# Placing 50,000 edges with one-hots of eight columns, columns innermost, in a four-layer graph network on one core

## The chip, the cores and the metric

The kernel runs on one core of a Trainium2 chip. The metric is the device time of one execution in microseconds (us), the median of several runs. TensorE (PE) multiplies matrices into PSUM, and its weight loads are listed as PEld; VectorE is DVE, ScalarE ACT, GpSimd POOL, SyncE SP.

## The reference

Four layers run on 3,125 nodes with 128 features and 50,000 edges (src, dst), edges sorted by dst. Each layer normalizes x, applies relu, gathers over edges and adds its result to x. Layers 0, 1 and 2 need the mean over incoming or outgoing edges, which this kernel takes from a dense count matrix A of the edges; layer 3 needs an attention over edges in both directions.

```python
msgs = x[row]
summed = jax.ops.segment_sum(msgs, col, num_segments=num_nodes)
count = jax.ops.segment_sum(jnp.ones((row.shape[0],), x.dtype), col, num_segments=num_nodes)[:, None]
agg = summed / jnp.maximum(count, 1.0)
...
edge_index = jnp.stack([src, dst])
h = jnp.maximum(_layernorm(x, axis=-1), 0.0)
x = x + _L0_gnn_ref(h, L0_gnn_W_lin, L0_gnn_W_agg, edge_index)
```

## The kernel before, in words

To build A, the edges are first sorted into 50 cells (25 tiles of 128 sources by two bands of 1,600 destinations). The input holds them as 125 partitions of EC = 400 columns. `place_dve` works out for each edge its place: a chunk number (0 to 447, `sort_v[:, 0]`) and a row in the chunk (0 to 127, `sort_v[:, 1]`), and two payloads of it, the destination and the source inside the cell, each plus one (`sort_v[:, 2]` and `[:, 3]`).

The stage of the change, "permute", moves the payloads to those places by matmuls. For every one of the 400 edge columns the weights are a one-hot of the row (128 wide) times a payload, the moving operand is a one-hot of the chunk (448 wide), and the product adds into PSUM bank 4 for one payload and bank 5 for the other: 800 matmuls of 448 columns in all, with 125 rows.

`permute_dve` handles U0 = 4 columns as a group. Per column it writes the chunk's one-hot into `A0` (L487, a comparison of `steps_h` with a per-partition scalar); for three columns (ACT_COLS) it writes the row's one-hot alone into `eq0` (L489); for the fourth it writes both products itself into `B0` (L492). `permute_act` multiplies the other three one-hots by both payloads (L513). `permute_pe` runs the group's eight matmuls (the helper `add_to`, L537). Operands of one column lie packed, and there are four buffers of each (g).

The signals: VectorE raises `eq_ready` after a group, ScalarE then `payload_ready`, TensorE `perm0_used` after its eight matmuls. VectorE waits for `perm0_used` of four groups before. After the last one it reads both banks (L502, L503) and raises `sorted_ready`, which opens the next stage, "build" (L558, L566, and L537 again), which makes A. There `oh_s` already holds eight columns innermost, made by one comparison (L566), and TensorE takes its weights from it as `oh_s[s][:, :, j]`, one f16 number in 16 bytes.

While the stage starts, GpSimd still runs `norm` for layer 0 with six instructions on the whole of h (L935 to L944). No DMA runs inside the stage.

Four lines elsewhere are read below for what they show of an access: L1251, a matmul whose moving operand `mrb[d][:, :, :, k]` takes 24 bf16 numbers from 24 rows of 416 or 448; L1176, a sum of two f32 results from bf16 columns of `sE`, 12 numbers (24 bytes) apart; L1374, a copy that writes `exs` 12 numbers apart; L1068, the same number of values in runs of 12. L739 is a packed cast of 1,024 numbers like L1375, and the matmuls of `exs` have 12 packed moving columns.

Of the kernel before, what the change touches and what calls it, by code (L numbers as in the profile page):

```python
# [7 lines left out]
F16 = mybir.dt.float16  # L8
BF16 = mybir.dt.bfloat16
I32 = mybir.dt.int32  # L10
ALU = mybir.AluOpType
ACT = mybir.ActivationFunctionType
AX_X = mybir.AxisListType.X

P = 128
# [4 lines left out]
EP = 125  # L20
EC = N_EDGES // EP
# [11 lines left out]
def chunk_bound(buckets):  # L33

    lap = LAP * GROUP
    return -(-((N_EDGES + buckets * (P - 1)) // P) // lap) * lap


CH = tuple(chunk_bound(b) for b in BUCKETS)
CHUNKS = max(CH)  # L40
# [48 lines left out]
def linker(eng, sem):  # L89

    count = [0]

    def link(ins):
        count[0] += 1
        ins.then_inc(sem, 1)
        eng.wait_ge(sem, count[0])

    return link


def gnn_kernel(nc, edges, x_in, consts, steps, weights, bias_cols, bias_rows, attn, out):
    with ExitStack() as ctx:
        def sb(name, shape, dt=F32):
            return ctx.enter_context(nc.sbuf_tensor(name, shape, dt))

        def sem(name):
            return ctx.enter_context(nc.semaphore(name))
# [5 lines left out]
        PS = ctx.enter_context(nc.psum_tensor("PS", [P, 8 * BANK], F32))  # L113
# [40 lines left out]
        exs = sb("exs", [P, 2, GROUP, SPLIT * HEADS], BF16)  # L154


        U0 = 4
        ACT_COLS = 3
        arena = sb("arena", [P, 29600])

        def view(at, width, rows=P):
            return arena[0:rows, at:at + width]
# [10 lines left out]
        def three(a):  # L173
# [13 lines left out]
        steps_h = view(26400, BW // 2).bitcast(F16)  # L187
        tabs = view(27200, CHUNKS + CELLS, 1).bitcast(I32)
        cell_turn, cell_end = tabs[:, 0:CHUNKS], tabs[:, CHUNKS:CHUNKS + CELLS]
        sort_v = view(23200, 4 * EC, EP).rearrange("p (a b) -> p a b", a=4)  # L190
# [1 line left out]
        packed = view(28800 + EC, EC, EP).bitcast(I32)  # L192
        back_i = view(28512, CH[0]).bitcast(I32)

        A0 = [view(g * U0 * CHUNKS // 2, U0 * CHUNKS // 2, EP).bitcast(F16).rearrange("p (j c) -> p j c", j=U0)
              for g in range(4)]
        B0 = view(3584, 16 * P, EP).bitcast(F16).rearrange("p (g j k c) -> p g j k c", g=4, j=U0, k=2)
        eq0 = view(5632, 8 * P, EP).bitcast(F16).rearrange("p (g j c) -> p g j c", g=4, j=U0)
        dst_in = view(6656, CH[1])

        RING_D, RING_S, RING_A = 4, 2, 4
# [2 lines left out]
                for s in range(RING_S)]  # L204
        stage = [view(11424 + s * BW // 2, BW // 2).bitcast(F16) for s in range(RING_A)]

        iota_8 = view(14624, GROUP * P // 2).bitcast(F16).rearrange("p (c j) -> p c j", j=GROUP)
        key_h = view(14624 + GROUP * P // 2, CHUNKS // 2).bitcast(F16)

# [65 lines left out]
        prod_ready, prod_used = sem("prod_ready"), sem("prod_used")  # L275
        placed, addr_ready = sem("placed"), sem("addr_ready")
        eq_ready, payload_ready, perm0_used = sem("eq_ready"), sem("payload_ready"), sem("perm0_used")
        sorted_ready = sem("sorted_ready")
        pads_written, scattered, order0_here = sem("pads_written"), sem("scattered"), sem("order0_here")
        order0_ready = sem("order0_ready")  # L280
# [56 lines left out]
        dve_link = linker(nc.vector, dve_step)  # L337
# [137 lines left out]
                t.matmul(PS[0:EP, SORT:SORT + EC], ident[0:EP, 0:EP], prod[:, n % PROD, :], start=(n == 0),  # L475
                         stop=(n == BUCKETS[d] - 1), skip_group_check=True).then_inc(prod_used, 1)

        LAPS0 = EC // (4 * U0)

        def permute_dve(v):  # L480

            def group(i, g, first=False):
                if not first:
                    v.wait_ge(perm0_used, 4 * i + g - 3)
                for j in range(U0):
                    c = bass.ds((4 * i + g) * U0 + j, 1)
                    v.tensor_scalar(A0[g][:, j, :], steps_h[0:EP, 0:CH[1]], sort_v[:, 0, c], None, ALU.is_equal)  # L487
                    if j < ACT_COLS:
                        last = v.tensor_scalar(eq0[:, g, j, :], steps_h[0:EP, 0:P], sort_v[:, 1, c], None, ALU.is_equal)  # L489
                    else:  # L490
                        for k in range(2):
                            last = v.tensor_scalar(B0[:, g, j, k, :], steps_h[0:EP, 0:P], sort_v[:, 1, c],  # L492
                                                   sort_v[:, 2 + k, c], ALU.is_equal, ALU.mult)
                last.then_inc(eq_ready, 1)

            for g in range(4):
                group(0, g, True)
            with v.Fori(1, LAPS0) as i:
                for g in range(4):
                    group(i, g)  # L500
            v.wait_ge(perm0_used, 4 * LAPS0)
            v.tensor_scalar(key[:, 1, :], PS[:, 5 * BANK:5 * BANK + CH[1]], -1.0, None, ALU.add)  # L502
            v.tensor_scalar(dst_in, PS[:, 4 * BANK:4 * BANK + CH[1]], -1.0, None, ALU.add).then_inc(sorted_ready, 1)  # L503

        def permute_act(a):

            with a.Fori(0, LAPS0) as i:
                for g in range(4):
                    a.wait_ge(eq_ready, 4 * i + g + 1)
                    for j in range(ACT_COLS):  # L510
                        for k in range(2):
                            c = bass.ds((4 * i + g) * U0 + j, 1)
                            last = a.activation(B0[:, g, j, k, :], eq0[:, g, j, :], ACT.Copy, scale=sort_v[:, 2 + k, c])  # L513
                    last.then_inc(payload_ready, 1)

        def permute_pe(t):
            for k in (4, 5):
                clear_bank(t, k)
            with t.Fori(0, LAPS0) as i:
                for g in range(4):  # L520
                    t.wait_ge(payload_ready, 4 * i + g + 1)
                    for j in range(U0):
                        for k in range(2):
                            at = (4 + k) * BANK
                            last = add_to(t, PS[:, at:at + CH[1]], B0[:, g, j, k, :], A0[g][:, j, :])
                    last.then_inc(perm0_used, 1)

        def clear_bank(t, k, n=BANK):
            t.matmul(PS[:, k * BANK:k * BANK + n], zeros[:, 0:P], zeros[:, 0:n], start=True, stop=False,
                     skip_group_check=True)  # L530
# [5 lines left out]
        def add_to(t, where, lhsT, rhs):  # L536
            return t.matmul(where, lhsT, rhs, start=False, stop=True, skip_group_check=True)  # L537
# [948 lines left out]
        def _(v):  # L1486
# [6 lines left out]
            v.wait_ge(loaded_steps, 16)  # L1493
            v.nop().then_inc(placed, 1)
            permute_dve(v)
            build_dve(v)

# [114 lines left out]
        def _(t):  # L1612
# [15 lines left out]
            place_sum_pe(t, 1, 0, CELLS)  # L1628
            t.wait_ge(placed, 1)
            permute_pe(t)  # L1630
            build_pe(t)
            t.wait_ge(slot_free, BANDS + CELLS)
# [93 lines left out]
        def _(a):  # L1726
            a.wait_ge(wx_summed, 1)
            a.copy(Wx[:, :], PS[:, 6 * BANK:6 * BANK + SC]).then_inc(wx_ready, 1)
            norm_act(a, 0)
            a.wait_ge(placed, 1)  # L1730
            permute_act(a)
            build_act(a)
            a.wait_ge(h_ready, 1)
# [105 lines left out]
```

## Time and profile before

| | us |
|---|---|
| three runs | 3679.42, 3669.36, 3679.49 (median 3679.42) |
| the profiled execution | 3675.2 |
| its span | 3673.1 |
| PE busy | 2217.1 (60%) |
| DVE busy | 2275.1 (62%) |
| ACT busy | 834.8 (23%) |
| POOL busy | 1652.6 (45%) |
| L513, 600 products | 186.1 busy |
| L487, 400 comparisons of 448 | 160.2 busy |
| L537, 4,320 matmuls of several stages | 781.0 busy |

The profile is of one execution. Busy is the time in which an engine had an instruction under way; instructions of one engine overlap at their ends, so a duration is longer than the distance from one to the next. A line number is that of the kernel before.

### The profile page before, as it was taken

To read this page: it belongs to the slowest core of one execution; us is meant where nothing else is said; L and a number is where in the kernel's file an instruction comes from. 1 tells how busy PE (TensorE), PEld (TensorE's weight loads), DVE (VectorE), ACT (ScalarE), POOL (GpSimd) and SP (SyncE) were. 2 spreads that over 40 slices of the span, in tenths; PEclk is the share of its full clock that TensorE was granted. 3 is DMA by queue.
4 is the path that set the end of the run, shared out by engine and by line. 5 is a ranking of instruction groups with operands and counts; after the bars stand their busy time and mean duration, and the time that the engine had idled before them with its cause. 6 is when DMAs were issued, how large, how long until landed. Compare 5 with 4: busy or idle time off the path is not lost.

```text
span 3673.1 us, 46525 instructions
## 1 busy us (share of the span) xinstructions
PE 2217.1 (60%) x12603; PEld 1303.9 (35%) x12659; DVE 2275.1 (62%) x3122; ACT 834.8 (23%) x1389; POOL 1652.6 (45%) x1455
## 2 busy tenths in 40 slices
PE   0688777778968999857333333334557554336663
PEld 0333545544534555524311111112456211115563
DVE  8999888885497003532233334337577896349877
ACT  0198333320012001120000100002334221004442
POOL 7300333330477777740266666657644666630000
PEclk9799999999979999979555555555589897555797
DMA  2000111114434342044433333332367333320352
GB/s 65 0 0 0 45 45 45 45 40 135 125 108 117 87 100 42 1 96 102 67 90 89 91 93 90 90 86 74 88 206 232 101 88 96 88 48 0 107 176 85
DMA packets 195114, 301.51 MB, mean 82 GB/s; under 512 B 120540, under 2 KB 133818, under 8 KB 194922
## 3 DMA queue, kind: packets, MB, share of 16 engines
q1 hardware_dynamic: 138986, 175.88, 15.1%
q0 software_dynamic: 40512, 62.87, 9.2%
q10 hardware_dynamic: 15552, 61.94, 5.6%
q8 instruction: 36, 0.59, 0.1%
q14 instruction: 28, 0.23, 0.0%
HBM read 191.65 MB, written 88.01 MB: 76 GB/s over the span
## 4 chain that ended last, share of the span: by engine, by line
PE 28%; DMA 24%; issue 17%; DVE 15%; POOL 9%; ACT 5%; ACTq 0%; DVEq 0%; SPq 0%; POOLq 0%; PEldq 0%
DMA arena<-T_att,idx 23%; PE PS L537 10%; POOL arena L1304 9%; PE PS L698 6%; PE PS L883 6%; ACT arena L513 3%; DVE arena L558 3%; PE PS L972 3%; DVE arena L1195 1%; DVE arena L373 1%; PE PS L475 1%; DVE arena L489 1%; PE PS L959 1%; DMA T_att<-parts 0%; DVE arena L566 0%
## 5 line engine op out<-in xcount | busy, mean ns | idle before, releaser
L1304 POOL DMA_INDIRECT arena<-T_att,idx x864 | 843.2, 976 | 627.8 <-DMA arena<-T_att,idx 457.5
L537 PE MATMUL PS<-arena 128*128 128x400 f16 (+2 forms) x4320 | 781.0, 331 | 266.1 <-issue 106.0
L1139 DVE TENSOR_REDUCE arena<-PS 128x1024 f32 (+1 forms) x432 | 504.7, 1216 | 582.5 <-PE PS L1106 562.3
L537 PEld LDWEIGHTS PS<-arena 128*128 128x128 f16 (+2 forms) x4320 | 528.3, 158 | 509.1 <-issue 350.0
L1477 POOL DMA_INDIRECT order<-arena x400 | 513.3, 1283 | 252.4 <-issue 252.4
L1095 PE MATMUL PS<-ident_b,score_buf 128*32 128x128 bf16 x864 | 96.2, 279 | 552.9 <-ACT score_buf L1068 542.0
L1106 PE MATMUL PS<-arena,pick 128*128 128x512 bf16 x812 | 340.5, 525 | 139.7 <-DVE arena L1139 107.1
L558 DVE TENSOR_SCALAR arena<-arena 128x1600 f16<-128x1600 f16 x448 | 381.1, 896 | 59.8 <-PE PS L537 55.6
L698 PE MATMUL PS<-arena 128*128 128x512 f16 (+1 forms) x1575 | 318.7, 362 | 95.5 <-issue 82.1
L632 POOL TENSOR_TENSOR rdeg<-rdeg,arena 128x1600 f32<-128x1600 f32 x48 | 160.1, 3337 | 307.0 <-ACT arena L616 307.0
L1095 PEld LDWEIGHTS PS<-ident_b,score_buf 128*32 128x32 bf16 x864 | 71.3, 124 | 625.3 <-issue 554.7
L698 PEld LDWEIGHTS PS<-arena 128*128 128x128 bf16 x1575 | 148.0, 99 | 262.2 <-issue 111.2
L513 ACT ACTIVATE arena<-arena 125x128 f16<-125x128 f16 x600 | 186.1, 388 | 79.0 <-DVE arena L492 73.6
L1106 PEld LDWEIGHTS PS<-arena,pick 128*128 128x128 bf16 x864 | 65.3, 111 | 362.1 <-DVE arena L1139 279.7
L1241 PE MATMUL PS<-ident_b,arena 128*128 128x128 bf16 x864 | 110.8, 309 | 134.5 <-issue 76.4
L1351 DVE TENSOR_TENSOR arena<-PS,key 128x1024 f32<-128x1024 f32 x108 | 132.3, 1225 | 90.5 <-PE PS L537 82.9
L1068 ACT COPY score_buf<-h 128x96 bf16 (+1 forms) x52 | 14.1, 271 | 665.8 <-POOL h L1313 665.8
L487 DVE TENSOR_SCALAR arena<-arena 125x448 f16<-125x448 f16 x400 | 160.2, 417 | 0.5 <-PE PS L537 0.5
L1273 ACT COPY arena<-PS 128x1024 bf16<-128x1024 bf16 x108 | 109.1, 1012 | 208.1 <-PE PS L1241 160.4
L883 PE MATMUL PS<-arena 128*128 128x400 f16 x800 | 147.0, 337 | 10.8 <-DVE arena L860 8.8
L616 ACT CAST arena<-PS 128x1600 f16<-128x1600 f32 x50 | 74.6, 1492 | 339.7 <-PE PS L537 339.7
L972 PE MATMUL PS<-arena,W 128*128 (+1 forms) x384 | 136.3, 514 | 20.9 <-DVE arena L1002 10.2
(258 smaller groups left out, 2797.6 us busy)
## 6 DMA issues: line engine op xcount, KB each, us to landing
spill<-arena SPq DMA_DIRECT2D x108, 560.0 KB
arena<-spill ACTq DMA_DIRECT2D x108, 560.0 KB
arena<-A SPq DMA_DIRECT2D x50, 800.0 KB
A<-arena SPq DMA_DIRECT2D x50, 400.0 KB, 2.4
arena<-A SPq DMA_DIRECT2D x50, 400.0 KB
arena<-T_att,idx POOLq DMA_INDIRECT x864
order<-arena POOLq DMA_INDIRECT x400
T_att<-h SPq DMA_DIRECT2D x2, 1600.0 KB, 13.9
```

What stands on the lines that cost most here:

```text
L487: v.tensor_scalar(A0[g][:, j, :], steps_h[0:EP, 0:CH[1]], sort_v[:, 0, c], None, ALU.is_equal)
L513: last = a.activation(B0[:, g, j, k, :], eq0[:, g, j, :], ACT.Copy, scale=sort_v[:, 2 + k, c])
L537: return t.matmul(where, lhsT, rhs, start=False, stop=True, skip_group_check=True)
L558: v.tensor_scalar(oh_d[s], steps_h, dst_in[:, bass.ds(RING_D * i + s, 1)], None, ALU.is_equal) \
L698: last = t.matmul(PS[:, a0:a1], narrow[s][:, k, :], strips[g % RING][:, a0:a1], start=(k == 0 and s == 0), stop=(k == TILES - 1 and s == S ...
L883: last = t.matmul(PS[:, at:at + w], wide[c][s][:, k, :], halves[n % HALVES][:, q * w:(q + 1) * w], start=(k == 0 and s == 0), stop=(k == T ...
L972: last = t.matmul(o, wt(name, c * H1 + ob * P), rhs, start=(n == 0), stop=(n == len(terms) - 1))
L1095: last = t.transpose(bank[:, j * P:(j + 1) * P], score_buf[:, half, j, :], ident_b[:, :])
L1106: last = t.matmul(PS[:, hd * BANK:(hd + 1) * BANK], pick[:, hd, :], sT[:, s:s + QUAD, :].rearrange("p j e -> p (j e)"), start=True, stop=True)
L1139: v.tensor_reduce(cmax[d][:, u:u + 2, bass.ds(i * SLOTS + half * GROUP + q // 2 * QUAD, QUAD)], PS[:, u * BANK:(u + 2) * BANK].rearrange(" ...
L1304: p.indirect_dma_start(out=ring1[:, b, j, :], out_offset=None, in_=T_att[d][:, :], in_offset=bass.IndirectOffsetOnAxis(ap=idx[:, d, k:k + ...
L1477: p.indirect_dma_start(out=order0[:, :], out_offset=bass.IndirectOffsetOnAxis(ap=addr[:, j:j + 1], axis=0), in_=packed[:, j:j + 1], in_off ...
```

## The change

U0 becomes 8, and there are two buffers in place of four. Two copies ahead of the loop write `iota_w` (each of the numbers 0 to 447 eight times, f16) and `sort_h` (places and payloads as f16). A unit of eight columns is then one comparison of 128 x 8 numbers (`eq0`), one of 448 x 8 (`A0`) and one product of 128 x 8 (`B0[g][0]`, the first payload) on VectorE, with the column as the innermost dimension of each; ScalarE makes `B0[g][1]`, the second payload, by eight products, one a column, reading and writing every eighth f16 number. TensorE waits for both and runs 16 matmuls whose weights and moving operand are every eighth number. VectorE waits for its own `eq_ready` before the product.

```diff
-        U0 = 4
-        ACT_COLS = 3
+        U0 = 8
...
+        def columns(at, n):
+            return view(at, n * U0 // 2, EP).bitcast(F16).rearrange("p (c j) -> p c j", j=U0)
+
+        A0 = [columns(g * CHUNKS * U0 // 2, CHUNKS) for g in range(2)]
+        B0 = [[columns(3584 + (2 * g + k) * P * U0 // 2, P) for k in range(2)] for g in range(2)]
+        eq0 = [columns(5632 + g * P * U0 // 2, P) for g in range(2)]
...
+            v.tensor_copy(iota_w, steps_h[0:EP, 0:CH[1]].unsqueeze(2).to_broadcast([EP, CH[1], U0]))
+            dve_link(v.tensor_copy(sort_h, sort_v))
+
+            def unit(i, g, first=False):
+                u = 2 * i + g
                 if not first:
-                    v.wait_ge(perm0_used, 4 * i + g - 3)
-                for j in range(U0):
-                    c = bass.ds((4 * i + g) * U0 + j, 1)
-                    v.tensor_scalar(A0[g][:, j, :], steps_h[0:EP, 0:CH[1]], sort_v[:, 0, c], None, ALU.is_equal)
...
+                    v.wait_ge(perm0_used, u - 1)
+                c = bass.ds(u * U0, U0)
+
+                def at(k, n):
+                    return sort_h[:, k, c].unsqueeze(1).to_broadcast([EP, n, U0])
+
+                v.tensor_tensor(eq0[g], iota_w[:, 0:P, :], at(1, P), ALU.is_equal).then_inc(eq_ready, 1)
+                v.tensor_tensor(A0[g], iota_w, at(0, CH[1]), ALU.is_equal)
+                v.wait_ge(eq_ready, u + 1)
+                v.tensor_tensor(B0[g][0], eq0[g], at(2, P), ALU.mult).then_inc(cols_ready, 1)
...
+                    a.wait_ge(eq_ready, u + 1)
+                    for j in range(U0):
+                        last = a.activation(B0[g][1][:, :, j], eq0[g][:, :, j], ACT.Copy,
+                                            scale=sort_v[:, 3, bass.ds(u * U0 + j, 1)])
                     last.then_inc(payload_ready, 1)
...
+                    t.wait_ge(cols_ready, u + 1)
+                    t.wait_ge(payload_ready, u + 1)
                     for j in range(U0):
                         for k in range(2):
                             at = (4 + k) * BANK
-                            last = add_to(t, PS[:, at:at + CH[1]], B0[:, g, j, k, :], A0[g][:, j, :])
+                            last = add_to(t, PS[:, at:at + CH[1]], B0[g][k][:, :, j], A0[g][:, :, j])
                     last.then_inc(perm0_used, 1)
```

VectorE, end of a group in the loop of the kernel before and the start of the next (ISA and REGISTER_ALU rows are register instructions; line numbers of each kernel's own):

```order
L489 TENSOR_SCALAR arena<-arena 125x128
L487 ISA
L487 TENSOR_SCALAR arena<-arena 125x448
L492 ISA
L492 TENSOR_SCALAR arena<-arena 125x128
L492 ISA
L492 TENSOR_SCALAR arena<-arena 125x128
L484 REGISTER_ALU
L487 ISA [waits perm0_used]
```

The changed kernel has this as one whole unit of eight columns at the same place:

```order
L498 ISA [waits perm0_used]
L498 TENSOR_TENSOR arena<-arena 125x1024
L499 ISA
L499 TENSOR_TENSOR arena<-arena 125x3584
L500 REGISTER_ALU
L501 ISA [waits eq_ready]
L501 TENSOR_TENSOR arena<-arena 125x1024
L498 ISA [waits perm0_used]
```

Two waits for TensorE and 18 comparisons and products become one wait for TensorE, one for VectorE itself and three instructions.

TensorE in the loop, two groups of the kernel before:

```order
L537 MATMUL PS<-arena 128x448 [waits payload_ready]
L537 MATMUL PS<-arena 128x448 x7
L521 REGISTER_ALU
L537 MATMUL PS<-arena 128x448 [waits payload_ready]
L537 MATMUL PS<-arena 128x448 x7
```

And two units of the changed one:

```order
L545 MATMUL PS<-arena 128x448 [waits payload_ready,cols_ready]
L545 MATMUL PS<-arena 128x448 x15
L528 REGISTER_ALU
L545 MATMUL PS<-arena 128x448 [waits payload_ready,cols_ready]
L545 MATMUL PS<-arena 128x448 x15
```

The number of matmuls and their size stay, with a wait at every sixteenth in place of every eighth, now for both engines' products.

## Rows read from the trace of the kernel before

**Rows 1.** Stretch, length, busy us of PE, PEld, DVE, ACT, POOL; granted clock; DMA.

```profile
250.00:300.00 50.00, 44.01 (x211) 18.28 (x210) 50.00 (x237) 48.53 (x157) 0.00 (x0) 1.00 0.00 0
```

**Rows 2.** Groups of instructions, 200 to 350 us: count, busy us, mean ns, idle before.

```profile
L513 ACT ACTIVATE arena<-arena 125x128 f16<-125x128 f16 x471 | 146.2, 388 | 4.4
L537 PE MATMUL PS<-arena 125*128 125x448 f16 x628 | 132.5, 354 | 18.2 <-ACT arena L513 18.2
```

**Rows 3.** Timeline near 251.5 us: start, length, instruction, count, idle before.

```profile
251.47 0.98 ACT L513 ACTIVATE arena<-arena 125x128 f16<-125x128 f16 x3
...
251.47 1.69 PE L537 MATMUL PS<-arena 125*128 125x448 f16 x8 [0.23 <-ACT arena L513]
253.39 1.69 PE L537 MATMUL PS<-arena 125*128 125x448 f16 x8 [0.23 <-ACT arena L513]
```

**Rows 4.** Timeline of the stage's start and end.

```profile
132.16 8.30 POOL L935 TENSOR_SCALAR h<-h 128x3200 f32<-128x3200 f32 x1 [40.76 <-DVE st L1492]
140.54 5.54 POOL L936 TENSOR_TENSOR h<-h,st 128x3200 f32<-128x3200 f32 x1
...
158.54 6.24 POOL L944 TENSOR_TENSOR arena<-rdeg,arena 128x3200 bf16<-128x3200 f32 x1
...
157.82 2.42 PE L537 MATMUL PS<-arena 125*128 125x448 f16 x6 [25.37 <-ACT arena L513]
...
354.17 0.69 DVE L492 TENSOR_SCALAR arena<-arena 125x128 f16<-125x128 f16 x2
358.65 0.62 DVE L502 TENSOR_SCALAR key<-PS 128x448 f32<-128x448 f32 x1 [3.79 <-PE PS L537]
```

**Rows 5.** Timeline of VectorE in the next stage.

```profile
366.28 0.68 DVE L566 TENSOR_TENSOR arena<-arena 128x1024 f16<-128x1024 f16 x1
366.88 0.63 DVE L558 TENSOR_SCALAR arena<-arena 128x1600 f16<-128x1600 f16 x1
```

**Rows 6.** Line L537 in three stretches: ns min/median/max, first and last start; then timeline.

```profile
L537 PEld LDWEIGHTS PS<-arena x627: 95/98/99, 199.9 to 349.8; 125*128 125x128 f16 x157
...
L537 PEld LDWEIGHTS PS<-arena x152: 140/143/152, 362.4 to 399.0; 128*128 128x128 f16 x152
...
L537 PEld LDWEIGHTS PS<-exs,arena x40: 95/96/100, 3445.5 to 3458.8; 128*128 128x128 bf16 x40
L537 PE MATMUL PS<-exs,arena x40: 167/168/179, 3445.6 to 3458.8; 128*128 128x12 bf16 x40
...
3451.87 0.32 PE L537 MATMUL PS<-exs,arena 128*128 128x12 bf16 x7
```

**Rows 7.** Line L1251: timeline; the line's ns; its stretch with the granted clock.

```profile
3390.31 0.45 PE L1251 MATMUL PS<-arena 128*128 x6
...
L1251 PE MATMUL PS<-arena x864: 201/218/230, 2535.7 to 3422.8; 128*128 x160, 128*128 128x24 bf16 x13
...
3380.00:3425.00 45.00, 16.35 (x224) 15.64 (x224) 0.50 0.00 0
```

**Rows 8.** VectorE: line L1176 twice, and a group of the same size, packed.

```profile
L1176 DVE TENSOR_TENSOR arena<-h x1: 3080/3080/3080, 2511.9 to 2511.9; 128x1664 f32<-128x1664 bf16 x1
L1176 DVE TENSOR_TENSOR arena<-W x1: 3304/3304/3304, 3309.6 to 3309.6; 128x1792 f32<-128x1792 bf16 x1
...
L1173 DVE SCALAR_TENSOR_TENSOR arena<-arena 128x1792 f32<-128x1792 f32 x1 | 2.0, 2026 | 0.0
```

**Rows 9.** ScalarE: three lines' ns min/median/max, and the timeline of one pair.

```profile
L1374 ACT COPY exs<-arena x108: 613/625/634, 2686.2 to 3619.7; 128x96 bf16 x100, 128x96 bf16<-128x96 bf16 x8
...
L1068 ACT COPY score_buf<-W x56: 264/265/273, 2862.7 to 3277.5; 128x96 bf16 x54, 128x96 bf16<-128x96 bf16 x2
...
L739 ACT CAST arena<-arena x6: 1039/1046/1155, 1041.8 to 1600.6; 128x1024 bf16<-128x1024 f32 x4, 128x1152 bf16<-128x1152 f32 x2
...
3450.56 0.62 ACT L1374 COPY exs<-arena 128x96 bf16 x1 [1.58 <-DVE arena L1351]
3450.74 1.29 ACT L1375 CAST arena<-arena 128x1024 bf16<-128x1024 f32 x1
```

More of the change, by code:

```diff
@@ L193, in gnn_kernel @@
         back_i = view(28512, CH[0]).bitcast(I32)
[L195 to L198, printed above, removed]
+        def columns(at, n):
[3 more added lines that the diff above has]
+        eq0 = [columns(5632 + g * P * U0 // 2, P) for g in range(2)]
         dst_in = view(6656, CH[1])
@@ L205, in gnn_kernel @@
         stage = [view(11424 + s * BW // 2, BW // 2).bitcast(F16) for s in range(RING_A)]
+        iota_w = columns(7200, CHUNKS)
+        sort_h = view(9000, 2 * EC, EP).bitcast(F16).rearrange("p (a b) -> p a b", a=4)
         iota_8 = view(14624, GROUP * P // 2).bitcast(F16).rearrange("p (c j) -> p c j", j=GROUP)
@@ L277, in gnn_kernel @@
         eq_ready, payload_ready, perm0_used = sem("eq_ready"), sem("payload_ready"), sem("perm0_used")
+        cols_ready = sem("cols_ready")
         sorted_ready = sem("sorted_ready")
@@ L476, in place_sum_pe @@
                          stop=(n == BUCKETS[d] - 1), skip_group_check=True).then_inc(prod_used, 1)
-        LAPS0 = EC // (4 * U0)
+        UNITS0 = EC // U0
         def permute_dve(v):
-            def group(i, g, first=False):
+            v.tensor_copy(iota_w, steps_h[0:EP, 0:CH[1]].unsqueeze(2).to_broadcast([EP, CH[1], U0]))
+            dve_link(v.tensor_copy(sort_h, sort_v))
+            def unit(i, g, first=False):
+                u = 2 * i + g
                 if not first:
-                    v.wait_ge(perm0_used, 4 * i + g - 3)
-                for j in range(U0):
-                    c = bass.ds((4 * i + g) * U0 + j, 1)
-                    v.tensor_scalar(A0[g][:, j, :], steps_h[0:EP, 0:CH[1]], sort_v[:, 0, c], None, ALU.is_equal)
[L488 to L501, printed above, removed]
+                    v.wait_ge(perm0_used, u - 1)
[6 more added lines that the diff above has]
+                v.tensor_tensor(B0[g][0], eq0[g], at(2, P), ALU.mult).then_inc(cols_ready, 1)
+            for g in range(2):
+                unit(0, g, True)
+            with v.Fori(1, UNITS0 // 2) as i:
+                for g in range(2):
+                    unit(i, g)
+            v.wait_ge(perm0_used, UNITS0)
             v.tensor_scalar(key[:, 1, :], PS[:, 5 * BANK:5 * BANK + CH[1]], -1.0, None, ALU.add)
@@ L505, in permute_act @@
         def permute_act(a):
[L507 to L513, printed above, removed]
+            with a.Fori(0, UNITS0 // 2) as i:
+                for g in range(2):
+                    u = 2 * i + g
+                    a.wait_ge(eq_ready, u + 1)
+                    for j in range(U0):
+                        last = a.activation(B0[g][1][:, :, j], eq0[g][:, :, j], ACT.Copy,
+                                            scale=sort_v[:, 3, bass.ds(u * U0 + j, 1)])
                     last.then_inc(payload_ready, 1)
@@ L518, in permute_pe @@
                 clear_bank(t, k)
-            with t.Fori(0, LAPS0) as i:
-                for g in range(4):
-                    t.wait_ge(payload_ready, 4 * i + g + 1)
+            with t.Fori(0, UNITS0 // 2) as i:
+                for g in range(2):
+                    u = 2 * i + g
+                    t.wait_ge(cols_ready, u + 1)
+                    t.wait_ge(payload_ready, u + 1)
                     for j in range(U0):
```

## The prediction

> **What bounds the stage now.** I read the busy time by stretches first, to find the stage in which the change works and whether its engines are full; then the groups of instructions and the timeline inside it, for the rhythm; then its two ends; and last the rest of the trace, for places where an engine already reads or writes lone 16-bit numbers, because that is what the new layout makes ScalarE and TensorE do.
>
> [...] One group of four edge columns repeats every 253.39 - 251.47 = 1.92 us [rows 3], so eight columns, one unit of the new code, cost 3.84 us. TensorE needs (1.69 - 0.35) / 7 = 0.19 us for each of its matmuls of 448 columns, 1.53 us of a group, and then waits for ScalarE [rows 2, 3]. ScalarE starts its products every (0.98 - 0.39) / 2 = 0.295 us [rows 2, 3]. [...] The stage is paid in full on the path: its first matmul stands at 157.82, VectorE's last one-hot at 354.17, and L502, which waits for the last matmul and opens the next stage, at 358.65 [rows 4].
>
> **The change, part by part.**
>
> VectorE: 18 instructions per eight columns go, three come. The comparison of 128 x 8 numbers has an exact twin in the next stage, 366.88 - 366.28 = 0.60 us [rows 5], and the product has the same size. The comparison of 448 x 8 is 3.5 times as large: 2.1 us at most. Together 3.3 us in place of 3.84. The wait on eq_ready inside the unit costs nothing, since the 2.1 us comparison lies between the producer and the waiting product. The two new copies ahead of the loop, of 3,584 and 1,600 numbers, are 2.1 and 0.9 us by the rate of rows 5 (an estimate: it is a comparison's), once. They fall into the time when GpSimd's large instructions, from 132.16 to 164.78, let VectorE through only in their gaps [rows 4], and they push the rest back by about one gap.
>
> ScalarE: 8 products per unit in place of 12, but each now reads and writes 128 numbers 16 bytes apart. The nearest row is L1374, a copy of 96 numbers that writes each 24 bytes from the last: 625 ns, where L1068 with 96 numbers side by side takes 265 [rows 9]. That is 360 ns more, 3.7 ns a number. The pair L1374, L1375 bounds it from below: both end at 3450.74 + 1.29 = 3452.03, 1.47 us after the start, the second alone is 1.05 (L739), so the first held the engine for 0.42, where L1068's kind would hold it for 0.27 - 0.09 = 0.18 (0.09 is how far two products overlap, 0.388 - 0.295): 240 ns, 2.5 a number [rows 2, 9]. For 128 numbers a product takes 0.295 + 0.32 to 0.47 = 0.61 to 0.77 us, a unit 4.9 to 6.1 us. The lower end, were 16 bytes apart free, is 8 x 0.295 = 2.4.
>
> TensorE: the same 800 matmuls, but both operands are now read with one 16-bit number in each 16 bytes. For the weights the next stage shows it: a load at 16 bytes takes 143 ns, a packed one 98 [rows 6], and 45 ns disappear behind a matmul. For the moving operand the trace of before has no row at 16 bytes, so I bound it. At the low end it is free: 0.19 us a matmul. A middle end is 45 ns for 128 columns as in the load, 0.35 ns each: 0.19 + 0.16 = 0.35 us. [...] I take **1.8 ns**: 448 x 1.8 = 806 ns a matmul, 12.9 us a unit of 16.
>
> That puts everything else out of sight: with two buffers VectorE (3.3) and ScalarE (4.9 to 6.1) prepare a unit within the 12.9 us of the one before, and the loads hide behind the matmuls.
>
> [...]
>
> **The sum.** Start: first copy at 132.0 to 134.1, second behind L935 (8.3 us) to 143.4, L936 (5.5) to 149, first comparison to 149.6, ScalarE's eight products to about 155. TensorE then runs 50 x 12.9 = 645 us without a gap, to 800, and L502 starts at about 800.4 in place of 358.65: +442 us. Nothing else is changed, and nothing outside runs beside the stage that would gain. The profiled execution took 3675.2 us (4 below the median of the three runs, 3679.4; its span is 3673.1): 3675 + 442 = **4117 us**. By itself this case runs from 1.75 ns (+424, 4099) to 1.92 ns a column (+485, 4160).
>
> **The rivals.**
>
> 1. *ScalarE becomes the bound, the moving read is free.* For: L1374 is the same engine, a 2-byte write to lone places. Against: rows 7 and 8. ScalarE starts at 149.6, 50 x (4.9 to 6.1, plus 0.15 for the wait of a unit) = 252 to 312, then the last unit's matmuls, 3.4: L502 at 405 to 465, +46 to +106, so 3721 to 3781, middle 3750.
>
> 2. *The moving read pays like the load*, 0.35 us a matmul, 5.5 us a unit. With two buffers and ScalarE at 5.5, two units take 0.7 + 5.5 + 5.5, a unit 5.9: 155 + 295 = 450, +92, 3767. For: it is the only row at exactly 16 bytes. [...]
>
> 3. *16 bytes apart costs nothing.* [...] Then VectorE's fewer instructions count: its 3.3 and TensorE's 3.1 us alternate over two buffers with some 0.4 us of signals, (3.3 + 3.1 + 0.4) / 2 = 3.4 us a unit. GpSimd, held up by some 11 us of VectorE's longer instructions in its gaps, ends at 164.8 + 11 = 176 with two units done: 176 + 48 x 3.4 + 0.5 = 340, -19 us, 3656. It decides from 4.0 us a unit downward, (358 - 158) / 50: a matmul must stay below 0.25 us (0.56 ns a column) and a product below 0.5. For: L566's layout, made for the same purpose, has strided weights that cost the next stage nothing. Against: those 45 ns in the load are there and only hidden. [...]
>
> That the change doesn't do what it says, a comparison at half the rate, is excluded by L566; even then VectorE would need 6.6 us, behind 12.9.
>
> **How the numbers follow.** My case 0.62; rival 1 0.14; rival 2 0.12; rival 3 0.10; 0.02 for something near no change. The prediction is my case, 4117 us. Its own range holds 0.62 at most, so the range takes in rivals 2 and 1: from 3735 to 4165. Faster by over 0.3% (about what a measurement of this kernel can tell from none): 0.10; within it: 0.02; slower: 0.88.
>
> **What would show it.** In the changed profile the matmuls of the stage (L545) should start 0.8 us apart with no wait between units, TensorE the only full engine, and the stage should last to about 800 us. VectorE's three instructions should stand at 0.6, 1.9 to 2.1 and 0.6 us with idle time behind TensorE's perm0_used, ScalarE's products at 0.6 to 0.8 us. I am wrong if matmuls start 0.19 or 0.35 us apart: then the lone read is cheap at 16 bytes, and whichever of ScalarE (idle time of TensorE behind L518) or VectorE is full names the rival.

## The result, and the profile after

| | before | changed |
|---|---|---|
| median, us | 3679.45 (3669.36 to 3682.3, 4 runs) | 4110.0 (4105.79 to 4119.2, 4 runs) |
| the profiled execution | 3675.2 | 4119.2 |
| its span | 3673.1 | 4117.1 |
| end of the stage (VectorE reads bank 5) | 358.65 | 795.51 |

The change makes the kernel slower, by a ratio of 1.1186 [1.1166, 1.1205] (95% interval): 4110 us where 4117 were forecast. The stage ends 436.9 us later. What follows it takes 4117.1 - 795.5 = 3321.6 us in place of 3314.4; these 7 us are within what the runs of one kernel differ by, and are not explained further. Line numbers have moved: L537 is now L545 (a few other matmuls stay on a line L537), the first comparison is L498, the one of 448 x 8 L499, VectorE's product L501, ScalarE's L518, and L502 is L509.

The stretch that answers to [rows 1], in the middle of the longer stage; columns as there:

```profile
400.00:450.00 50.00, 50.00 (x64) 9.17 (x63) 12.91 (x12) 19.70 (x32) 0.00 (x0) 0.50 0.00 0
```

VectorE falls from 50 us of 50 to 13 and ScalarE from 48.5 to 20, while TensorE, at 44 before, is never idle. It starts 64 matmuls in 50 us where it started 211. The groups that answer to [rows 2], from 200 to 780 us:

```profile
L545 PE MATMUL PS<-arena 125*128 125x448 f16 x731 | 580.9, 975 | 0.0
L518 ACT ACTIVATE arena<-arena 125x128 f16<-125x128 f16 x367 | 226.2, 1052 | 350.2 <-DVE arena L498 350.2
L545 PEld LDWEIGHTS PS<-arena 125*128 125x128 f16 x730 | 106.3, 146 | 473.6 <-issue 473.6
L499 DVE TENSOR_TENSOR arena<-arena 125x3584 f16<-125x3584 f16 x46 | 92.8, 2018 | 0.0
L501 DVE TENSOR_TENSOR arena<-arena 125x1024 f16<-125x1024 f16 x46 | 31.5, 684 | 0.0
L498 DVE TENSOR_TENSOR arena<-arena 125x1024 f16<-125x1024 f16 x45 | 31.1, 692 | 426.7 <-PE PS L545 426.7
```

The matmul's idle time is 0.0. VectorE has stood idle for 426.7 us before L498, each time behind TensorE (the wait for `perm0_used`), and ScalarE's 350.2 us behind L498 are that same wait handed on. One unit in the timeline, to set beside [rows 3]:

```profile
399.70 13.69 PE L545 MATMUL PS<-arena 125*128 125x448 f16 x17
401.64 0.69 DVE L498 TENSOR_TENSOR arena<-arena 125x1024 f16<-125x1024 f16 x1 [9.48 <-PE PS L545]
402.25 2.02 DVE L499 TENSOR_TENSOR arena<-arena 125x3584 f16<-125x3584 f16 x1
402.47 4.92 ACT L518 ACTIVATE arena<-arena 125x128 f16<-125x128 f16 x8 [7.78 <-DVE arena L498]
```

Seventeen matmuls take 13.69 us. Each record is 0.98 us long and overlaps the next, so it is (13.69 - 0.98) / 16 = 0.794 us from one start to the next, 1.77 ns a column, where it was 0.19 us. A unit of 16 takes 12.7 us and its operands are ready after some 5.8 (402.47 + 4.92 - 401.64), so TensorE alone sets the rhythm. Products on ScalarE start (4.92 - 1.05) / 7 = 0.55 us apart.

The start and the end of the stage, to set beside [rows 4]:

```profile
131.61 1.96 DVE L486 COPY arena<-arena 125x3584 f16<-125x3584 f16 x1
131.79 9.94 POOL L943 TENSOR_SCALAR h<-h 128x3200 f32<-128x3200 f32 x1 [40.22 <-DVE st L1500]
133.49 9.08 DVE L487 CAST arena<-arena 125x1600 f16<-125x1600 f32 x1
141.81 6.15 POOL L944 TENSOR_TENSOR h<-h,st 128x3200 f32<-128x3200 f32 x1
142.61 5.90 DVE L498 TENSOR_TENSOR arena<-arena 125x1024 f16<-125x1024 f16 x1
...
148.43 4.67 DVE L499 TENSOR_TENSOR arena<-arena 125x3584 f16<-125x3584 f16 x1
148.66 4.86 ACT L518 ACTIVATE arena<-arena 125x128 f16<-125x128 f16 x8 [56.75 <-DVE arena L498]
151.30 7.89 POOL L950 TENSOR_TENSOR rdeg<-h,arena 128x3200 f32<-128x3200 f32 x1
...
153.02 6.72 DVE L501 TENSOR_TENSOR arena<-arena 125x1024 f16<-125x1024 f16 x1
...
159.79 2.59 PE L545 MATMUL PS<-arena 125*128 125x448 f16 x3 [27.71 <-DVE arena L501]
...
795.51 0.62 DVE L509 TENSOR_SCALAR key<-PS 128x448 f32<-128x448 f32 x1 [22.06 <-PE PS L545]
```

VectorE's first unit is slow beside GpSimd's large instructions: 9.08, 5.90 and 6.72 us for instructions that take 0.9 (an estimate by the rate of L486, 1.96 us for 3,584 numbers), 0.69 and 0.68 us alone. Each of the three ends with one of GpSimd's, within 0.9 us; no run takes GpSimd's away. ScalarE's eight products are done at 148.66 + 4.86 = 153.52, but VectorE's own product L501 runs beside GpSimd's L950 until 159.7, and the first matmul waits for it. In the kernel before, three comparisons of 128 that take 0.24 us alone end with GpSimd's L935, L936 and L941 (8.30, 5.54 and 2.85 us) in the same way:

```profile
132.14 8.36 DVE L489 TENSOR_SCALAR arena<-arena 125x128 f16<-125x128 f16 x1
...
140.54 5.58 DVE L489 TENSOR_SCALAR arena<-arena 125x128 f16<-125x128 f16 x1
...
146.29 2.86 DVE L489 TENSOR_SCALAR arena<-arena 125x128 f16<-125x128 f16 x1
```

### The profile page after: what moved, and what is told of

It is laid out like the page before. It is cut to its first block, busy times and chain, and to the rows that moved or that the text cites. A ratio compares the mean times of both kernels' runs of the same rounds, so it can differ in the third digit from the quotient of the medians.

```text
span 4117.1 us, 44607 instructions
## 1 busy us (share of the span) xinstructions
PE 2692.1 (65%) x12603; PEld 1352.1 (33%) x12659; DVE 2249.8 (55%) x2374; ACT 895.2 (22%) x1189; POOL 1656.3 (40%) x1455
## 4 chain that ended last, share of the span: by engine, by line
PE 44%; DMA 23%; DVE 14%; issue 10%; POOL 8%; ACT 1%; DVEq 0%; SPq 0%; POOLq 0%; ACTq 0%; PEldq 0%
PE PS L545 24%; DMA arena<-T_att,idx 22%; POOL arena L1312 8%; PE PS L706 8%; PE PS L891 5%; DVE arena L566 3%; PE PS L980 3%; PE PS L479 1%; DVE arena L1203 1%; PE PS L967 1%; DVE arena L377 1%; DMA T_att<-parts 0%; DVE arena L574 0%; PE PS L1249 0%; DVE arena L997 0%
## 5 line engine op out<-in xcount | busy, mean ns | idle before, releaser
L545 PE MATMUL PS<-arena 128*128 128x400 f16 (+2 forms) x4320 | 1242.1, 445 | 241.3 <-issue 114.4
L545 PEld LDWEIGHTS PS<-arena 128*128 128x128 f16 (+2 forms) x4320 | 569.8, 165 | 903.4 <-issue 861.1
L566 DVE TENSOR_SCALAR arena<-arena 128x1600 f16<-128x1600 f16 x448 | 391.6, 917 | 65.7 <-PE PS L545 62.0
L518 ACT ACTIVATE arena<-arena 125x128 f16<-125x128 f16 x400 | 246.3, 1051 | 437.8 <-DVE arena L498 437.8
L498 DVE TENSOR_TENSOR arena<-arena 125x1024 f16<-125x1024 f16 x50 | 42.4, 849 | 446.9 <-PE PS L545 446.8
```

What stands on the lines that cost most here:

```text
L518: last = a.activation(B0[g][1][:, :, j], eq0[g][:, :, j], ACT.Copy, scale=sort_v[:, 3, bass.ds(u * U0 + j, 1)])
L566: v.tensor_scalar(oh_d[s], steps_h, dst_in[:, bass.ds(RING_D * i + s, 1)], None, ALU.is_equal) \
```

## The experiments

All kernels but the last two are the changed one with the edit named; the kernel before ran beside them at 3656 to 3673 us (medians of each set). Runs 2, 3, 4, 6 and 7 are one execution each, so a few us between two of them mean nothing by themselves. The end of the stage is given with each, since there the effect stands alone: 358.65 before, 795.51 in the changed kernel.

### 1. Moving operand packed

`A0` is laid out column after column again, written by eight comparisons; all else stays.

```diff
-                v.tensor_tensor(A0[g], iota_w, at(0, CH[1]), ALU.is_equal)
+                for j in range(U0):
+                    v.tensor_scalar(A0[g][:, j, :], steps_h[0:EP, 0:CH[1]], sort_v[:, 0, bass.ds(u * U0 + j, 1)], None, ALU.is_equal)
...
-                            last = add_to(t, PS[:, at:at + CH[1]], B0[g][k][:, :, j], A0[g][:, :, j])
+                            last = add_to(t, PS[:, at:at + CH[1]], B0[g][k][:, :, j], A0[g][:, j, :])
```

> The change with A0, the moving operand, packed again (eight per-column comparisons in place of the one of 448 x 8); weights and products keep 16 bytes between numbers. Theory 1 (a lone 16-bit number of the moving operand costs 1.77 ns, whatever the weights do): matmuls 0.19 us apart, ScalarE's eight products (4.9 us a unit) set the rhythm at 5.05 us, the stage ends at about 405 us in place of 795, some 3720 us in all, and TensorE's granted clock leaves 0.50 for most of the stage. Theory 2 (the spaced weights are the cost): matmuls stay at 0.79 us, about 4110 us. [...]

Measured: 3711.4 us (3700.15 to 3731.12), ratio to before 1.0132 [1.0089, 1.0175]; the stage ends at 416.8. Timeline, the matmuls of two units:

```profile
301.58 3.22 PE L546 MATMUL PS<-arena 125*128 125x448 f16 x16 [1.46 <-ACT arena L519]
...
306.23 3.22 PE L546 MATMUL PS<-arena 125*128 125x448 f16 x16 [1.42 <-ACT arena L519]
```

Sixteen matmuls stand (3.22 - 0.35) / 15 = 0.19 us apart again, although the weights are still read at 16 bytes, and TensorE waits for ScalarE. Its groups from 220 to 320 us:

```profile
L519 ACT ACTIVATE arena<-arena 125x128 f16<-125x128 f16 x161 | 95.0, 1063 | 7.8 <-DVE arena L498 7.8
L546 PE MATMUL PS<-arena 125*128 125x448 f16 x311 | 69.7, 384 | 29.4 <-ACT arena L519 29.3
```

So 378.7 of the 436.9 us go when the moving operand is packed. Behind it ScalarE's spaced products are the next limit. Eight take 4.65 us in the timeline (306.23 against 301.58) and 8 x 100 / 161 = 4.97 on average over the 100 us; 50 x (4.97 - 3.84) = 57 us, about the other 58. The end at 416.8 lies 12 us behind the 405 expected. That the average lies above 4.65 goes with a granted clock below 1.00 early in the stage: there packed matmuls take longer and buffers come free later. In the unit at 190.19, at 0.50, sixteen take 6.16 us and the first thirteen 5.05, so each takes (6.16 - 5.05) / 3 = 0.37, 0.83 ns a column. From 300 us on, at 1.00, ScalarE has no idle time. This link is argued, not tested:

```profile
190.19 6.16 PE L546 MATMUL PS<-arena 125*128 125x448 f16 x16 [2.93 <-ACT arena L519]
...
200.00:250.00 50.00, 35.52 (x135) 20.07 (x136) 28.68 (x90) 43.15 (x74) 0.00 (x0) 0.80 0.00 0
```

### 2. Weights packed, moving operand spaced

`B0` is laid out column after column for both payloads; `A0` stays as in the changed kernel. The first payload's product on VectorE then reads `eq0` in a turned order.

```diff
-                v.tensor_tensor(B0[g][0], eq0[g], at(2, P), ALU.mult).then_inc(cols_ready, 1)
+                v.tensor_tensor(B0[g][0], eq0[g].rearrange("p c j -> p j c"),
+                                sort_h[:, 2, c].unsqueeze(2).to_broadcast([EP, U0, P]), ALU.mult).then_inc(cols_ready, 1)
...
-                        last = a.activation(B0[g][1][:, :, j], eq0[g][:, :, j], ACT.Copy,
+                        last = a.activation(B0[g][1][:, j, :], eq0[g][:, :, j], ACT.Copy,
...
-                            last = add_to(t, PS[:, at:at + CH[1]], B0[g][k][:, :, j], A0[g][:, :, j])
+                            last = add_to(t, PS[:, at:at + CH[1]], B0[g][k][:, j, :], A0[g][:, :, j])
```

> The change with B0, the weights, packed for both payloads and A0 left at 16 bytes. Theory 1: matmuls stay at 0.79 us, about 4110 us, loads 98 ns warm or 150 at the half clock. Theory 2: matmuls at 0.19 to 0.37 us, 3720 to 3770 us. ScalarE now reads at 16 bytes and writes packed: if the write is what makes a product 0.58 us, it falls to about 0.3 us; if the read does, it stays near 0.58.

Measured: 4098.1 us, end of the stage 790.6. Groups, 220 to 320 us:

```profile
L546 PE MATMUL PS<-arena 125*128 125x448 f16 x129 | 101.7, 965 | 0.0
L519 ACT ACTIVATE arena<-arena 125x128 f16<-125x128 f16 x64 | 27.2, 508 | 73.5 <-DVE arena L498 73.5
...
L501 DVE TENSOR_TENSOR arena<-arena 125x1024 f16<-125x1024 f16 x8 | 15.6, 1947 | 0.0
```

A matmul still takes 101.7 / 129 = 0.79 us; the stage ends 5 us earlier of 437. A packed load takes 123 ns here, at granted clock 0.50, where a spaced one takes 146; expected were 150. The run also gives two side prices. ScalarE's product that reads spaced and writes packed takes (3.40 - 0.51) / 7 = 0.41 us, not 0.55, which is neither of the two values expected:

```profile
300.71 3.40 ACT L519 ACTIVATE arena<-arena 125x128 f16<-125x128 f16 x8 [9.18 <-DVE arena L498]
```

And VectorE's product, now written packed from spaced input and a payload repeated along its innermost dimension, takes 1.95 us instead of 0.68: the changed kernel's form of it is the fast one.

### 3, 4 and 6. The distance: 8, 4 and 32 bytes

`A0` is written in blocks of four or two columns (3 and 4), so that every read takes every fourth or second number, or with eight numbers of every sixteen used (6). The edit of 3 (W0 is 2 in 4), and that of 6:

```diff
+        W0 = 4
+        A0 = [view(g * CHUNKS * U0 // 2, CHUNKS * U0 // 2, EP).bitcast(F16).rearrange("p (q c j) -> p q c j", c=CHUNKS, j=W0)
+              for g in range(2)]
...
+                for q in range(U0 // W0):
+                    w = bass.ds(u * U0 + q * W0, W0)
+                    v.tensor_tensor(A0[g][:, q], iota_w[:, :, 0:W0], sort_h[:, 0, w].unsqueeze(1).to_broadcast([EP, CH[1], W0]),
+                                    ALU.is_equal)
```

```diff
-        A0 = [columns(g * CHUNKS * U0 // 2, CHUNKS) for g in range(2)]
+        A0 = [view(at, 8 * CHUNKS, EP).bitcast(F16).rearrange("p (c j) -> p c j", j=16)[:, :, 0:U0] for at in (0, 9800)]
```

> The change with A0 in two blocks of four columns, so that the moving operand's numbers are 8 bytes apart, two to each 16 bytes. Theory 1a (the price is one of each new 16 bytes): 1.77 / 2 = 0.89 ns a column, 0.40 us a matmul, 6.4 us a unit, about 3790 us. Theory 1b (only a lone number in its 16 bytes pays): 0.19 us a matmul, then ScalarE's 5.05 us a unit, about 3720 us.

> The change with A0 in four blocks of two columns, numbers 4 bytes apart, four to each 16 bytes. Theory 1a: 1.77 / 4 = 0.44 ns a column, 0.20 us a matmul; theory 1b: 0.19 us. Either way ScalarE sets the rhythm, about 3720 us. Should spacing as such cost, whatever the number in 16 bytes, matmuls would stay near 0.79 us.

> The change with A0's numbers 32 bytes apart (every second 16 bytes left empty). A price per new 16 bytes, whatever the distance: matmuls stay 0.79 us apart, about 4110 us. A price for distance, or for neighbouring places that come cheaper than far ones: 1.9 ns a column or more as in L1251, 0.85 us a matmul, 4155 us or above.

Measured: 3793.8, 3716.3 and 4118.5 us; the stage ends at 489.0, 412.0 and 805.7. The matmul groups, 220 to 320 us, at 8, 4 and 32 bytes:

```profile
L550 PE MATMUL PS<-arena 125*128 125x448 f16 x251 | 101.0, 582 | 0.0
```

```profile
L550 PE MATMUL PS<-arena 125*128 125x448 f16 x335 | 71.8, 365 | 28.7 <-ACT arena L523 28.7
```

```profile
L545 PE MATMUL PS<-arena 125*128 125x448 f16 x125 | 101.1, 987 | 0.0
```

At 4 bytes TensorE waits again, so the timeline gives its rate:

```profile
303.24 3.42 PE L550 MATMUL PS<-arena 125*128 125x448 f16 x16 [1.32 <-ACT arena L523]
```

| distance of neighbours | one matmul of 448, us | ns a column | ns for each new 16 bytes |
|---|---|---|---|
| 2 bytes (packed) | 0.19 | 0.43 | (3.4) |
| 4 bytes | 0.204 | 0.46 | (1.8) |
| 8 bytes | 0.402 | 0.90 | 1.80 |
| 16 bytes | 0.794 | 1.77 | 1.77 |
| 32 bytes | 0.81 | 1.81 | 1.81 |

From 16 to 32 bytes almost nothing is added, from 16 to 8 the price halves. But the granted clock differs too: it is 0.50 at 16 and 32 bytes and 1.00 in run 3's stretch. So a rival fits the table as well: a column at 8 bytes or more apart costs about twice a packed one at the same granted clock, whatever the distance (0.90 ns against 0.43 at 1.00, 1.77 against run 1's 0.83 at 0.50), and the clock makes the factor of two. Run 3's own start decides. From 173 to 179 us its clock is 0.50, from 183 to 189 it is 1.00:

```profile
173.65 5.81 PE L550 MATMUL PS<-arena 125*128 125x448 f16 x14 [5.19 <-ACT arena L523]
...
182.49 7.01 PE L550 MATMUL PS<-arena 125*128 125x448 f16 x17
...
173.00:179.00 6.00, 5.35 (x14) 2.09 (x15) 1.29 (x2) 5.17 (x9) 0.00 (x0) 0.50 0.00 0
183.00:189.00 6.00, 6.00 (x17) 2.15 (x16) 2.88 (x5) 4.54 (x9) 0.00 (x0) 1.00 0.00 0
```

That is (5.81 - 0.58) / 13 = 0.402 us a matmul at the low level and (7.01 - 0.58) / 16 = 0.402 at the high one. The rival would have 0.8 at the low one. So the two levels can be compared: it is a price per 16 bytes that a stream opens, about 1.8 ns, and no price per number or per distance. At 4 bytes four numbers share it, 1.8 / 4 = 0.45 ns, hardly above the packed rate. With two numbers in each 16 bytes (8 bytes apart) a matmul still takes twice the packed time (0.402 us against 0.19), and with one (16 bytes apart) four times (0.794).

### 7. Spaced write alone

`A0` packed as in 1, and `eq0` packed too, by eight comparisons, so that ScalarE reads packed and only its write is spaced.

```diff
-                        last = a.activation(B0[g][1][:, :, j], eq0[g][:, :, j], ACT.Copy,
+                        last = a.activation(B0[g][1][:, :, j], eq0[g][:, j, :], ACT.Copy,
```

> A0 and eq0 packed, the products of both payloads written at 16 bytes, so that ScalarE reads packed and writes spaced. Read and write prices add (0.295 packed, 0.41 read spaced, 0.58 both): 0.295 + 0.17 = 0.465 us a product, 3.9 us a unit for ScalarE. The slower one hides the other: 0.58 us, as in the change. VectorE has 8 more comparisons and a product that reads far apart, some 5.2 us a unit, and sets the rhythm: about 3730 us. TensorE: 0.19 us a matmul.

Measured: 3758.0 us, end 447.9. ScalarE and VectorE's product, groups 220 to 320 us:

```profile
L521 ACT ACTIVATE arena<-arena 125x128 f16<-125x128 f16 x144 | 88.8, 1059 | 13.0 <-DVE arena L499 13.0
...
L504 DVE TENSOR_TENSOR arena<-arena 125x1024 f16<-125x1024 f16 x18 | 35.1, 1952 | 0.0
```

The record of a product is 1059 ns, as with both spaced (1063 in run 1) and against 508 in run 2; eight in the timeline take 4.94 us, 0.55 from one to the next. So the write sets ScalarE's price, (0.55 - 0.295) / 128 = 2.0 ns a number, and the read, 0.9 ns a number by itself (0.41 - 0.295 over 128), hides behind it. The run is slower than run 1 because VectorE now needs 5.2 us for a unit (16 comparisons, 1.3 and 2.0, and this product, 1.9), and all three engines wait for one another a little (144 products in 100 us, 5.6 us a unit). The granted clock is 0.86 from 250 to 350 us, as in run 1 early on. The end, 3758 for the 3730 expected, was not taken apart further.

### 5. A mixed version

Each operand in the form that its reader or writer takes well: the moving one-hot packed; the first payload by one product of 128 x 8, columns innermost, because a spaced weight load is hidden (in run 1 the matmuls stand 0.19 us apart with it); the second written packed by ScalarE.

```diff
-        B0 = [[columns(3584 + (2 * g + k) * P * U0 // 2, P) for k in range(2)] for g in range(2)]
+        B0 = [[columns(3584 + 2 * g * P * U0 // 2, P),
+               view(3584 + (2 * g + 1) * P * U0 // 2, P * U0 // 2, EP).bitcast(F16).rearrange("p (j c) -> p j c", j=U0)]
+              for g in range(2)]
...
+                            w = B0[g][1][:, j, :] if k else B0[g][0][:, :, j]
+                            last = add_to(t, PS[:, at:at + CH[1]], w, A0[g][:, j, :])
```

> The change with A0 packed (as in e1) and the second payload's products written packed by ScalarE, which still reads every eighth number; the first payload's products stay columns innermost on VectorE. From e2 a product that only reads at 16 bytes stands 0.41 us from the next, so ScalarE needs 8 x 0.41 + 0.15 = 3.4 us a unit; VectorE 0.6 + 8 x 0.245 + 0.6 = 3.2; TensorE 3.1, so that two buffers allow (3.2 + 3.1 + 0.4) / 2 = 3.35. A unit of 3.45 us against 3.84 in the kernel before: the stage ends at about 340 us in place of 359, 15 to 22 us below the kernel before, ratio 0.994 to 0.996. Against it: if TensorE's packed moving operand beside spaced weights costs more in a full rhythm, or the loop over two buffers adds more than 0.4 us of signals, a unit is 3.8 us and the ratio 1.00.

Measured: 3685.8 us (9 runs), ratio 1.0028 [1.0018, 1.0038], end 365.5. The expected gain did not come. Groups, 220 to 320 us:

```profile
L521 ACT ACTIVATE arena<-arena 125x128 f16<-125x128 f16 x205 | 89.2, 518 | 11.6 <-DVE arena L500 11.0
L549 PE MATMUL PS<-arena 125*128 125x448 f16 x407 | 82.2, 354 | 18.2 <-ACT arena L521 18.2
...
L500 DVE TENSOR_TENSOR arena<-arena 125x1024 f16<-125x1024 f16 x26 | 18.0, 693 | 17.1 <-PE PS L549 17.1
```

No engine is full, and the granted clock is 1.00. Each waits for the next in a circle: TensorE for ScalarE, ScalarE for VectorE's L500, L500 for TensorE. One lap in the timeline:

```profile
252.28 0.69 DVE L500 TENSOR_TENSOR arena<-arena 125x1024 f16<-125x1024 f16 x1 [1.09 <-PE PS L549]
...
253.11 6.97 ACT L521 ACTIVATE arena<-arena 125x128 f16<-125x128 f16 x16 [0.88 <-DVE arena L500]
...
256.72 3.22 PE L549 MATMUL PS<-arena 125*128 125x448 f16 x16 [1.12 <-ACT arena L521]
...
260.11 0.69 DVE L500 TENSOR_TENSOR arena<-arena 125x1024 f16<-125x1024 f16 x1 [1.08 <-PE PS L549]
```

It takes 260.11 - 252.28 = 7.83 us: comparison 0.7, eight products 3.5, sixteen matmuls 3.2, and the remaining 0.4 between the end of one and the start of the next. With two buffers a unit takes half, 3.9: what is seen, 16 matmuls every 100 x 16 / 407 = 3.93 us. The expectation had put VectorE and TensorE alone into that lap, 3.35 us, and left ScalarE's products out of it. The step from four small buffers to two large ones, which the change also makes, had a price that the other costs covered.

### 8 and 9. Four buffers and two, units of four columns

Run 8 is run 5 with U0 = 4 and four buffers (`RING0`) in the same memory (`iota_w` is needed only 128 wide); run 9 is run 8 with two buffers and nothing else.

```diff
-        U0 = 8
+        U0, RING0 = 4, 4
...
-                u = 2 * i + g
+                u = RING0 * i + g
...
-                    v.wait_ge(perm0_used, u - 1)
+                    v.wait_ge(perm0_used, u - RING0 + 1)
```

> The mixed version (moving one-hots packed by one comparison a column, the first payload's products with the columns innermost on VectorE, the second's written packed by ScalarE) with units of four columns over four buffers instead of eight over two. Theory, the loop over two buffers is what held the mixed version at 3.9 us per eight columns: with four buffers the slowest engine sets the rhythm, VectorE at 0.4 + 4 x 0.245 + 0.35 = 1.7 us per four columns or ScalarE at 4 x 0.42 = 1.7 us, so 3.4 to 3.6 us per eight columns; the stage of 50 x 3.5 = 175 us ends near 340, some 16 to 24 us earlier than in the kernel before, and the ratio to it is 0.993 to 0.996. Rival, the engines slow each other down when all work on packed and spaced numbers at once (or each short comparison of four columns costs a fixed start): 3.9 us per eight columns again, ratio 1.000 to 1.004.

> The four-buffer version with two buffers in place of four, units still of four columns, nothing else. In the four-buffer run ScalarE's products stood 0.31 us apart instead of 0.42 in the mixed version of eight columns (it now reads numbers 8 bytes apart, not 16), so two things had changed at once. If the number of buffers was the limit: the loop eq0 0.4 + ScalarE 1.3 + TensorE 1.6 + three signals 0.3 over two buffers is 1.8 to 1.9 us per four columns, with idle time of VectorE behind perm0_used; the stage's end is at 345 to 358 and the ratio to the kernel before 0.996 to 1.001. If the distance of 8 bytes alone made the difference: 1.65 us per four columns as with four buffers, VectorE always busy, end at 331, ratio 0.991 to 0.993.

Measured: run 8 3628.0 us (3625.05 to 3630.14, 5 runs), ratio to before 0.9918 [0.9905, 0.9932], end 330.8. Run 9 3657.0 us, ratio 1.0006 [0.9994, 1.0019], end 359.9. Groups of run 8, 220 to 320 us:

```profile
L549 PE MATMUL PS<-arena 125*128 125x448 f16 x485 | 100.4, 353 | 0.0
L521 ACT ACTIVATE arena<-arena 125x128 f16<-125x128 f16 x243 | 80.2, 401 | 20.4 <-DVE arena L500 20.4
L502 DVE TENSOR_SCALAR arena<-arena 125x448 f16<-125x448 f16 x244 | 64.4, 318 | 0.0
...
L504 DVE TENSOR_TENSOR arena<-arena 125x512 f16<-125x512 f16 x60 | 24.4, 406 | 0.0
L500 DVE TENSOR_TENSOR arena<-arena 125x512 f16<-125x512 f16 x60 | 24.3, 405 | 0.0
```

And of run 9:

```profile
L549 PE MATMUL PS<-arena 125*128 125x448 f16 x414 | 87.1, 353 | 13.3 <-ACT arena L521 10.9
...
L500 DVE TENSOR_TENSOR arena<-arena 125x512 f16<-125x512 f16 x52 | 22.1, 425 | 9.9 <-PE PS L549 8.2
```

With four buffers VectorE's three instructions have no idle time before them. L549 shows none either, but its records overlap: before each group the weight load waits 0.4 us for VectorE's L504. So VectorE sets the rhythm.

```profile
252.90 1.27 PEld L549 LDWEIGHTS PS<-arena 125*128 125x128 f16 x8 [0.38 <-DVE arena L504]
```

Four columns take 100 / 60.6 = 1.65 us, 3.30 for eight (3.4 to 3.6 were expected) where the kernel before takes 3.84. With two, the circle of run 5 is back (L500 behind TensorE) and four columns take 100 / 51.8 = 1.93, a little more than the 1.8 to 1.9 expected. The number of buffers alone is worth 29 us. Since these units are of four columns, ScalarE reads at 8 bytes instead of 16, and its products stand (1.32 - 0.40) / 3 = 0.31 us apart, close to packed ones:

```profile
251.47 1.32 ACT L521 ACTIVATE arena<-arena 125x128 f16<-125x128 f16 x4 [0.33 <-DVE arena L500]
```

Run 9 has that too and gains nothing from it, so the gain of run 8 needs the buffers. Run 8 beats both kernels: the stage ends 27.9 us earlier than before.

## Why the prediction was right

*Which case.* The forecast was that the moving operand's reading would bound the stage; runs 1 and 2 show it by taking one operand back at a time. Rival 1's price exists as well, but only as what is left once the moving read is cheap: run 1, at 3711 us with the stage ending at 416.8, is its case (405 to 465), with TensorE waiting for ScalarE as it says. Rivals 2 and 3 have no support left: the moving read costs 0.60 us more a matmul, not 0.16 and not nothing. Rival 2 took a load's 45 ns for a moving operand's: at granted clock 1.00, 128 spaced columns cost the load 47 ns more (145 in run 3 against 98 before), while 128 moving ones cost (1.77 - 0.43) x 128 = 172, the 1.77 measured at 0.50 and the 0.43 at 1.00. Why a load pays less is not shown.

*The price.* The 1.8 ns a column of the sum, and its range of 1.75 to 1.92, no run shows at 16 bytes: what the runs show there is 1.77, and 1.81 at 32. They were my estimate from rows at 24 and over 800 bytes: 224 ns for 128 more numbers of L1176, 1.75 each (rows 8), and six matmuls of L1251 that start within 0.45 - 0.22 = 0.23 us, 46 ns for 24 columns, 1.92 each, at granted clock 0.50 (rows 7). What sets L1251's 46 ns is not shown: a register instruction of TensorE's queue on the same line takes 46 ns too (800 of them for 864 matmuls). The estimate took the distance not to matter, and from 16 to 32 bytes that held. It also took the price to be one per lone number; run 3 shows that it is per 16 bytes, and at 8 bytes the same formula would have been wrong by a factor of two. Of the two readers VectorE was a weak one: L1176 adds two spaced inputs, so its 1.75 ns pay for two lone numbers. That 1.8 came within 2% of 1.77 is in part luck, as the rows gave 1.75 and 1.92 and neither is at 16 bytes.

*The sum.* Expected 12.9 us a unit and an end at 800.4, +442; measured 12.7, 795.5, +437. Two errors cancel in part. The units were 0.2 us shorter, 10 us in all. The start was 5 us later, at 159.79 for 155: I had counted the copies and ScalarE's products behind GpSimd's first two instructions, but not VectorE's own product of the first unit, which runs beside L950 until 159.7. In the profiled execution 7 us more lie after the stage (4119.2 - 3675.2 = 444).

*VectorE.* 0.6, 2.0 and 0.6 us were expected and came (402.25 - 401.64 = 0.61; 2.02; 0.68 as a record), and it stood idle behind `perm0_used`.

*ScalarE.* Expected 0.61 to 0.77 us a product, measured 0.55, and 0.58 over a long run of them: 2.0 to 2.2 ns a number, below my 2.5 to 3.7. The term was too large, by a tenth at its low end, and hidden. The row behind it, L1374, was a copy of another type at 24 bytes; that its full price would apply was the weak point.

*What hid.* The wait on `eq_ready` cost nothing in the changed kernel, as said (idle time before L501: 0.0). The spaced weights cost next to nothing: the load is 23 ns longer at the clock of the changed kernel (146 against 123 in run 2), and the 5 us of run 2 are all that shows. That two buffers cost nothing was also said, and is right only behind a slow TensorE: runs 8 and 9 show 29 us for it once TensorE is fast. Rival 3's sum of 3.4 us a unit over two buffers can't be tested by run 5, where the lap goes through ScalarE's 3.5 us; with the 2.4 that this rival gave ScalarE, VectorE's 3.3 would be the longer way.

## What to carry to other kernels

Before an operand's innermost dimension is chosen for the engine that writes it, count how often it is read and by whom: here one write of 3,584 numbers is read by sixteen streams of 448. VectorE gained nothing even from the big comparison, since one of 448 x 8 takes 2.02 us and eight packed ones of 448 take 2.05, as this row of run 5's timeline shows; only the two small instructions were a saving (the comparison of 128 x 8 takes 0.69 us, eight of 128 in run 7 take 1.38), and those can be had with the moving operand packed.

```profile
252.88 2.05 DVE L502 TENSOR_SCALAR arena<-arena 125x448 f16<-125x448 f16 x8
```

When a group is made larger at the cost of the number of buffers, add up one lap around all the engines that hand the buffer on and divide by the number of buffers. In run 5 that was 7.8 / 2 = 3.9 us, more than the 3.5 of the slowest engine, ScalarE, and it was the bound: the profile showed three engines that each waited a little for the next.

## What the runs showed that I had not expected

*The granted clock with a busy TensorE.* From 200 us on, at 16 bytes, TensorE shows no idle time, and yet its granted clock is 0.50 in every stretch that was read up to 780 us (the row of 400 to 450 us stands above). At 32 bytes it is 0.50 as well. At 8 bytes, equally without a gap, it is 1.00:

```profile
200.00:250.00 50.00, 50.00 (x126) 18.06 (x125) 26.08 (x32) 39.21 (x64) 0.00 (x0) 1.00 0.00 0
```

So "busy" in the profile was no sign here of a granted clock of 1.00. By run 3 the low level, 0.50, costs a spaced stream nothing: 0.402 us a matmul at either level, at 8 bytes. At 16 bytes no stretch had the high level, so that it would be the same there is carried over from run 3. Why the level was low was not tried.

*ScalarE.* A packed product of 128 f16 numbers starts every 0.295 us, one read at 8 bytes every 0.31, read at 16 bytes 0.41, written at 16 bytes 0.55. The step comes between 8 and 16 bytes for the read; a write at 8 bytes was not tried.

*VectorE.* The product of 1,024 numbers takes 0.68 us with all operands running along the innermost dimension. In run 7 it writes packed and has the same second factor, and only `eq0` is read otherwise, each number 256 bytes from the last: 1.95 us, 1.9 ns a number. In run 2, with `eq0` read at 16 bytes, it is 1.95 as well. So a lone read costs VectorE about as much as TensorE, 1.9 against 1.77 ns. In run 2 the second factor also changes (it is repeated along the innermost dimension), and that adds nothing that shows.
